# Products of the identity with itself in TensorE's waits, in a two-layer vision tower

## Chip, cores and metric

The kernel runs on one core of one Trainium2 chip. The metric is the device time of one execution in microseconds (us), as the median of several runs. The kernel is one program that computes the whole tower; all stages share one set of engines: TensorE (PE, with its weight loads as PEld), VectorE (DVE), ScalarE (ACT), GpSimd (POOL) and SyncE (SP).

## The reference

64 images of 64x64x3 are cut into 16 patches each, which makes 1024 tokens of width 192. On them:

```
h = patches @ W + b + pos_emb
h = h + attn0(layernorm(h))       # 12 heads of 16, each image attends to its own 16 tokens, softmax, no output matrix
h = h + soft_moe(layernorm(h))    # 4 experts x 256 slots:
    logits   = x @ phi            #   (tokens, 1024 slots)
    dispatch = softmax over the image's 16 tokens; combine = softmax over the 1024 slots
    out      = combine @ mlp_e(dispatch.T @ x)
h = h + attn1(layernorm(h))       # 6 heads of 32, low-rank projections, rotary, causal
h = h + routed_moe(layernorm(h))  # 32 experts in 4 groups, 4 of them per token
```

All of it is in float32. The change touches only the first attention (attn0) and the computation of the slot weights (logits, dispatch and combine).

## The kernel before

**Stages.** `build` writes the stages one behind the other: `embed`, `attention0` (which begins with the layernorm "ln0"), the layernorm "ln1", `slot_weights`, `hidden_pieces`, `slot_experts`, `attention1`, `routed_moe`. Each stage is a block in which every engine has its own written-out list of instructions; the engines meet at the end of a block, so a stage begins when the slowest engine has ended the one before. Within a block the engines wait for each other on counting semaphores. There is no scheduler: the order on an engine is the order in which the code is written. The tokens are handled in 8 tiles of 128 (`TILES`, `P`).

**keep_busy** (line 92) already exists. `keep_busy(pe, g, bank, products)` issues that many float32 products of the 128x128 identity `g.ident` with itself into the first 128 columns of a PSUM bank; nobody reads them (line 95). The kernel before calls it at the start of `embed` (6 products, line 130) and in each layernorm before the transposes (16 products, line 202). In the trace one product is two records, each a weight load and a matmul of 128x128.

**attention0.** TensorE's list is, in order: queries and keys of the first 512 tokens in four parts, each two matmuls of 96x512 (`queries_and_keys(n)`, n = 0 to 3, line 388), with `values(0)` and `values(1)` among them (line 396); `scores(0)`, `scores(1)` (line 408); `values(2)`, `values(3)`; and then a loop over the tiles i = 0 to 7. In the loop stand:

- at i = 0 the parts n = 4 to 7 of the queries and keys of the other 512 tokens;
- `scores(i + 2)`, as long as there is such a tile; at i = 2 `values(4)` to `values(7)` come ahead of it, each of which waits until VectorE has taken the one before out of the only bank for values (`v_done`, line 518);
- `turn(i - 1)` (line 428), three transposes of the outputs of the tile before, after ScalarE has copied them to SBUF (`leave_outputs`, line 474);
- `outputs(i)` (line 419), 12 small products of probabilities and values, which wait for the exponentials of tile i.

After the loop comes `turn(7)`. ScalarE's list is the key copies of a part (`leave(5)`, six activations, line 467) and one query copy (line 464), for each tile four exponentials (line 485), and behind those of tile i the copy of the outputs of tile i-1. VectorE takes the other keys out (`leave(4)`, six operations, line 513), then for each tile the maximum, the subtraction and a transpose (`center`, lines 524 to 531), and at the end of a tile `finish` (lines 536 to 540); GpSimd adds the result to `h` (line 500).

**ln1** is `layernorm(..., wide=True)`: VectorE computes the statistics and `xn`, GpSimd copies 64 columns of each tile once more (line 170), TensorE transposes (line 209), ScalarE copies to `xnT` (line 225).

**slot_weights.** For each tile TensorE computes the logits (`logits`, lines 785 and 789), transposes them into `dl` and, one tile later, the normalised combine weights into `tp` (both line 778). The loop has 9 rounds; `logits(i + 2)` stands at the end of the rounds 0 to 5, and the rounds 6, 7 and 8 have nothing in its place. ScalarE copies `cl` and `tp` out (lines 816 and 835), computes two sets of exponentials (826, 838) and scales one of them (832); GpSimd multiplies the dispatch weights by the inverse sums (877). Then `hidden_pieces` begins, whose first work on TensorE is eight transposes (line 973) and products of 128x384 (lines 979 and 984).

The functions that the change touches:

Of the kernel before, what the change touches and what calls it, by code (L numbers as in the profile page):

```python
# [18 lines left out]
TILES = TOKENS // P  # L19
# [72 lines left out]
def keep_busy(pe, g, bank, products):  # L92

    for _ in range(products):
        pe.matmul(bank[:, 0:P], g.ident[:], g.ident[:], start=True, stop=True)
# [257 lines left out]
def attention0(nc, g, t):  # L353
# [4 lines left out]
    with Scope(nc, "at0") as s:  # L358
# [17 lines left out]
        def _(pe):  # L376
# [15 lines left out]
            def values(i):  # L392
                if i >= 1:
                    pe.wait_ge(v_done, i)
                for k in range(NKD):
                    mm = pe.matmul(vp[:, 0:D], g.xnT[:, k, i * P:(i + 1) * P], t.w[:, k, 2 * D:3 * D],
                                   start=(k == 0), stop=(k == NKD - 1))
                mm.then_inc(v_ready, 1)
# [38 lines left out]
            scores(0)  # L437
            scores(1)
            values(2)
            values(3)  # L440
            for i in range(TILES):
                if i == 0:
                    for n in range(4, 8):
                        queries_and_keys(n)
                if i + 2 < TILES and i != 2:
                    scores(i + 2)
                if i == 2:
                    for j in range(TILES // 2, TILES):
                        values(j)
                    scores(i + 2)  # L450
                if i >= 1:
                    turn(i - 1)
                outputs(i)
            turn(TILES - 1)

        @block.scalar
        def _(act):
# [285 lines left out]
def slot_weights(nc, g, CT, Dn, zn):  # L743


    with Scope(nc, "slw") as s:
# [4 lines left out]
        cl = s.ps("cl", [P, 2, 2, 512])  # L751
# [20 lines left out]
        @block.tensor  # L772
        def _(pe):
            pe.wait_ge(g.phi_in, 16)

            def transposed(bank, src, ready):
                for c in range(SLOT_CHUNKS):
                    tr = pe.transpose(chunks(bank)[:, c, :], src[:, c * P:(c + 1) * P], g.ident[:])
                tr.then_inc(ready, 1)

            def logits(i):
                if i >= 2:
                    pe.wait_ge(lg_ready, i - 1)
                for half in range(2):
                    pe.matmul(cl[:, i % 2, half, :], g.wideT[:, 0, i * P:(i + 1) * P], g.phi[:, half * 512:(half + 1) * 512],
                              start=True, stop=False)
                for half in range(2):
                    rows = slice(half * KQ, (half + 1) * KQ)
                    mm = pe.matmul(cl[:, i % 2, half, :], g.wideT[rows, 1, i * P:(i + 1) * P], g.phi[rows, ALL_SLOTS:],
                                   start=False, stop=True)  # L790
                mm.then_inc(cl_ready, 1)

            logits(0)
            logits(1)
            for i in range(TILES + 1):
                if i < TILES:
                    pe.wait_ge(lg_ready, i + 1)
                    if i >= 1:
                        pe.wait_ge(dsub_ready, i)
                    transposed(dl, lg[:, i % 2], dl_ready)  # L800
                if i >= 1:
                    pe.wait_ge(cw_ready, i)
                    if i >= 2:
                        pe.wait_ge(ct_done, i - 1)
                    transposed(tp, ex[:, (i - 1) % 2], tp_ready)
                if i + 2 < TILES:
                    logits(i + 2)

        @block.scalar
        def _(act):  # L810
# [1098 lines left out]
```

## Time and profile before

| | us |
|---|---|
| median of 3 runs | 1126.56 |
| lowest and highest run | 1112.64, 1131.46 |
| the profiled execution, its device time | 1124.79 |
| its span in the trace | 1123.0 |
| TensorE busy in the span | 996.8 (89%) |
| ScalarE busy | 666.5 (59%) |
| VectorE busy | 390.0 (35%) |
| mean granted clock of TensorE | 0.945 of full speed |

All times inside the program are counted from the start of the span. A row of a timeline gives the start of a group of like instructions, its length, the engine, the source line, the tile that is written and the ones that are read, the number of records, and in brackets how long the engine was idle before and who released it. Stages in this execution, by TensorE's first instruction: the attention's main block 32.3 to 88.9, ln1 to 98.2, slot weights to 155.5, hidden pieces after that.

### The profile page before, as it was taken

The page shows a single profiled execution, that of the slowest core. Times are in us where ns is not written, and L with a number is a line of the kernel's source. Part 1 is how long each engine was busy: PE and PEld are TensorE (multiplying, and loading weights), DVE is VectorE, ACT ScalarE, POOL GpSimd, SP SyncE. Part 2 cuts the span into 40 slices and gives each one's busy share as a digit, 9 for nine tenths or more (in the row PEclk, how much of TensorE's full clock was granted, in tenths as well). Part 3 has the DMA queues.
Part 4 walks back from the last instruction along what each step waited for, and adds up shares of the span by engine and source line. Part 5 has one row for each costly group of instructions (what it writes and reads, how often), then busy time and mean ns, then how long its engine had stood idle before and what let it go on. Part 6 is the DMA issues. An engine that isn't in the chain of part 4 may idle for free. (4 is left out here: it accounts for less than half of the span.)

```text
span 1123.0 us, 21359 instructions
## 1 busy us (share of the span) xinstructions
PE 996.8 (89%) x7464; PEld 653.3 (58%) x7464; DVE 390.0 (35%) x1021; ACT 666.5 (59%) x1226; POOL 257.4 (23%) x256
## 2 busy tenths in 40 slices
PE   8878769779999999999999997875159999999997
PEld 8345445433444445444444445444149999999996
DVE  2555968650011111111111113774832222222233
ACT  0474968679888888788888881262013443334332
POOL 0111233230000000000000000100455555655531
PEclk9888969889999999999999999997569999999999
DMA  9000008979545555445544511004369999999994
GB/s 356 7 1 1 1 30 318 315 315 187 118 114 127 123 118 119 109 121 125 124 112 116 113 29 47 0 1 136 140 224 286 323 328 328 325 320 334 321 267 127
DMA packets 76137, 185.52 MB, mean 165 GB/s; under 512 B 15888, under 2 KB 34544, under 8 KB 75768
## 3 DMA queue, kind: packets, MB, share of 16 engines
q1 hardware_dynamic: 63788, 169.45, 49.5%
q0 software_dynamic: 11808, 14.39, 6.2%
q8 instruction: 64, 1.05, 0.4%
q14 instruction: 45, 0.37, 0.1%
q10 hardware_dynamic: 432, 0.26, 0.1%
HBM read 148.37 MB, written 35.69 MB: 164 GB/s over the span
## 5 line engine op out<-in xcount | busy, mean ns | idle before, releaser
L1182 ACT ACTIVATE sle_H<-sle_hp 128x1024 f32<-128x1024 f32 x384 | 367.5, 1024 | 57.7 <-PE sle_hp L1119 57.6
L1631 ACT ACTIVATE ext_H<-ext_hp,ext_bias 128x128 f32<-128x128 f32 x378 | 103.9, 397 | 162.9 <-issue 159.2
L1136 PE MATMUL sle_up<-sle_H,sle_cw 128*32 128x512 f32 (+1 forms) x2048 | 191.4, 492 | 0.0
L1197 DVE STREAM_TRANSPOSE sle_UT<-sle_up 128x256 f32<-128x256 f32 x64 | 37.3, 583 | 291.7 <-PE sle_up L1136 291.7
L1576 PE MATMUL ext_yp<-rmoe_w,ext_H 128*128 128x192 f32 x756 | 133.5, 326 | 1.1 <-issue 0.6
L1576 PEld LDWEIGHTS ext_yp<-rmoe_w,ext_H 128*128 128x128 f32 x756 | 121.6, 191 | 1.6 <-issue 1.6
L1119 PE MATMUL sle_hp<-keep_G,keep_dT 99*128 99x512 bf16 (+1 forms) x512 | 101.8, 332 | 12.3 <-PEq L897 6.8
L1104 POOL COPY sle_cw<-keep_CT 128x128 f32 (+1 forms) x64 | 18.7, 293 | 393.0 <-PE sle_up L1136 392.9
L1136 PEld LDWEIGHTS sle_up<-sle_H,sle_cw 128*32 128x32 f32 x2048 | 53.5, 109 | 87.0 <-issue 73.4
L1119 PE MATMUL sle_hp<-sle_G,sle_dT 99*128 99x512 bf16 (+1 forms) x512 | 100.0, 327 | 1.1 <-ACT sle_H L1182 1.1
L1558 PE MATMUL ext_hp<-ext_xT,rmoe_w 128*128 128x128 f32 x756 | 97.2, 280 | 0.0
L1119 PEld LDWEIGHTS sle_hp<-keep_G,keep_dT 99*128 99x128 bf16 x512 | 44.8, 99 | 81.7 <-ACT sle_H L1182 31.3
L1558 PEld LDWEIGHTS ext_hp<-ext_xT,rmoe_w 128*128 128x128 f32 x756 | 91.9, 196 | 0.0
L1119 PEld LDWEIGHTS sle_hp<-sle_G,sle_dT 99*128 99x128 bf16 x512 | 44.5, 98 | 69.4 <-ACT sle_H L1182 30.3
L1735 POOL DMA_INDIRECT sum<-ext_y,ext_yi x40 | 63.6, 1589 | 61.7 <-DVE ext_gate L1653 33.5
L1724 POOL DMA_INDIRECT ext_x<-xn,ext_xi x63 | 61.9, 983 | 34.9 <-issue 26.6
L1145 PE MATMUL sle_up<-keep_w,sle_UT 128*128 128x192 f32 x384 | 67.3, 326 | 0.8 <-DVE sle_UT L1197 0.8
L1663 DVE COPY ext_yi<-rmoe_slot 128x1 uint32<-128x1 uint32 x63 | 9.7, 154 | 154.6 <-PE ext_yp L1576 152.2
L1145 PEld LDWEIGHTS sle_up<-keep_w,sle_UT 128*128 128x128 f32 x384 | 61.7, 190 | 2.1 <-DVE sle_UT L1197 1.7
L979 PE MATMUL hid_gps<-pre_w,vit_xnT 128*128 128x384 f32 x128 | 47.2, 512 | 5.7 <-DVE hid_rest L1022 5.7
L1564 PE MATMUL ext_hp<-ext_xT,rmoe_w 64*128 64x128 f32 x756 | 51.4, 283 | 0.0
L999 ACT ACTIVATE hid_gp<-hid_gps 128x768 bf16<-128x768 f32 (+1 forms) x40 | 34.0, 850 | 27.1 <-PE hid_gps L984 14.6
(271 smaller groups left out, 1213.6 us busy)
## 6 DMA issues: line engine op xcount, KB each, us to landing
rmoe_w<-W SPq DMA_DIRECT2D x126, 576.0 KB
pieces<-hid_gp SPq DMA_DIRECT2D x16, 1152.0 KB, 4.8
keep_G<-pieces SPq DMA_DIRECT2D x32, 288.0 KB, 3.9
sle_G<-pieces SPq DMA_DIRECT2D x32, 288.0 KB, 3.8
pieces<-hid_gp SPq DMA_DIRECT2D x8, 768.0 KB, 5.5
keep_G<-pieces SPq DMA_DIRECT2D x32, 192.0 KB, 3.8
sle_G<-pieces SPq DMA_DIRECT2D x32, 192.0 KB, 3.7
keep_CT<-xT SPq DMA_DIRECT2D x6, 512.0 KB, 6.5
```

Of the source, the lines that this page charges most:

```text
L979: pe.matmul(gps[(STEPS * i + e) % 4][:, half, 0:HALF], g.wideT[:, 0, tokens], g.w1[:, e - 1, half * HALF:(half + 1) * HALF], start=True, s ...
L1119: mm = pe.matmul(hp[k % DEEP][:, j, off:off + width], dT[b][:, c * P:(c + 1) * P], G[b][:, (c // 2) * HID + at:(c // 2) * HID + at + width ...
L1136: mm = pe.matmul(to[32 * e:32 * e + 32], cw[:, p, 2 * e + grp, :], H[:, p, h:h + width], start=(p == 0 and grp == 0), stop=(p == 1 and grp ...
L1145: mm = pe.matmul(yps, UT[:, par, b, :], g.w2[:, b, :], start=(b == blocks[0]), stop=(b == blocks[-1]))
L1182: act.activation(H[:, p, WIDTH * k:WIDTH * (k + 1)], hp[k % DEEP][:].rearrange("p a c -> p (a c)"), ACT.Gelu_apprx_tanh).then_inc(gelu_don ...
L1197: dve.transpose(UT[:, par, at // 32:(at + width) // 32, 32 * j:32 * j + 32], src.rearrange("p (b c) -> p b c", c=32)).then_inc(ut_done[ban ...
L1558: pe.matmul(hp[q][:, c % 2, (c // 2) * P:(c // 2 + 1) * P], rt.w1[:, w, c, :], xT[:, q, 0, :], start=(c < 2), stop=False)
L1564: mm = pe.matmul(hp[q][:, c % 2, (c // 2) * P:(c // 2 + 1) * P], rt.w1[rows, w, HC + c // 2, :], xT[rows, q, 1, :], start=False, stop=(c > ...
L1576: mm = pe.matmul(yp[:, 0:D], H[:, q, c, :], rt.w2[:, w, c, :], start=(c == 0), stop=(c == HC - 1))
L1631: act.activation(H[:, q, c, :], hp[q][:, c % 2, (c // 2) * P:(c // 2 + 1) * P], ACT.Gelu, bias=bias[:, q, c:c + 1]).then_inc(gelu_done, 1)
L1724: pool.indirect_dma_start(out=x[:, p, :], out_offset=None, in_=xn_dram, in_offset=bass.IndirectOffsetOnAxis(ap=xi[p][:], axis=0)).then_inc ...
L1735: pool.indirect_dma_start(out=sums[q], out_offset=bass.IndirectOffsetOnAxis(ap=yi[q][:], axis=0), in_=y[:, q, :], in_offset=None, compute_ ...
```

## The change

`keep_busy` is called at further places of two of TensorE's lists. In `attention0`: 9 products between `values(2)` and `values(3)`; 2 behind each of the parts 4, 5 and 6 of the queries and keys; 2 behind each of `values(4)` to `values(7)`; for the tiles 3, 4 and 5 two ahead of `outputs(i)` and two behind it, for the tiles 6 and 7 four and four; 12 behind `turn(7)`. In `slot_weights`: 8 at the end of each of the rounds 6, 7 and 8. The banks written are `oT` before any outputs exist, `qk[0]` once its last content has left, and halves of `cl` that have been read. No wait is added, and the other engines' lists stay as they are. All products are counted here as matmuls; the trace shows two records for each.

```
--- before.py
+++ after.py
@@ -437,21 +437,30 @@
             scores(0)
             scores(1)
             values(2)
+            keep_busy(pe, g, oT, 9)
             values(3)
             for i in range(TILES):
                 if i == 0:
                     for n in range(4, 8):
                         queries_and_keys(n)
+                        if n < 7:
+                            keep_busy(pe, g, oT, 2)
                 if i + 2 < TILES and i != 2:
                     scores(i + 2)
                 if i == 2:
                     for j in range(TILES // 2, TILES):
                         values(j)
+                        keep_busy(pe, g, qk[0], 2)
                     scores(i + 2)
                 if i >= 1:
                     turn(i - 1)
+                if i >= 3:
+                    keep_busy(pe, g, qk[0], 2 if i + 2 < TILES else 4)
                 outputs(i)
+                if i >= 3:
+                    keep_busy(pe, g, qk[0], 2 if i + 2 < TILES else 4)
             turn(TILES - 1)
+            keep_busy(pe, g, qk[0], 12)
 
         @block.scalar
         def _(act):
@@ -805,6 +814,8 @@
                     transposed(tp, ex[:, (i - 1) % 2], tp_ready)
                 if i + 2 < TILES:
                     logits(i + 2)
+                else:
+                    keep_busy(pe, g, cl[:, i % 2, 0], 8)
 
         @block.scalar
         def _(act):
```

On TensorE, in the first attention, from the values of the tiles 2 and 3 to the last part of the queries and keys (`at_w,vit_xnT` are values, `vit_xnT,at_w` queries and keys, `vit_ident` alone the added products):

```order
-L396 MATMUL at_b<-at_w,vit_xnT 128x192 x4
-L388 MATMUL at_b<-vit_xnT,at_w 96x512 x8
+L396 MATMUL at_b<-at_w,vit_xnT 128x192 x2
+L95 MATMUL at_b<-vit_ident 128x128 x9
+L396 MATMUL at_b<-at_w,vit_xnT 128x192 x2
+L388 MATMUL at_b<-vit_xnT,at_w 96x512 x2
+L95 MATMUL at_b<-vit_ident 128x128 x2
+L388 MATMUL at_b<-vit_xnT,at_w 96x512 x2
+L95 MATMUL at_b<-vit_ident 128x128 x2
+L388 MATMUL at_b<-vit_xnT,at_w 96x512 x2
+L95 MATMUL at_b<-vit_ident 128x128 x2
+L388 MATMUL at_b<-vit_xnT,at_w 96x512 x2
```

What stood in one piece is now cut by 9, 2, 2 and 2 products.

On TensorE, the end of the first attention, tiles 6 and 7 (`at_oT` are the transposes of outputs, `at_probT,at_v` the outputs):

```order
 L428 MATMUL at_b<-vit_ident,at_oT 128x128 x3
+L95 MATMUL at_b<-vit_ident 128x128 x4
 L419 MATMUL at_b<-at_probT,at_v 32x128 x12
+L95 MATMUL at_b<-vit_ident 128x128 x4
 L428 MATMUL at_b<-vit_ident,at_oT 128x128 x3
+L95 MATMUL at_b<-vit_ident 128x128 x4
 L419 MATMUL at_b<-at_probT,at_v 32x128 x12
+L95 MATMUL at_b<-vit_ident 128x128 x4
 L428 MATMUL at_b<-vit_ident,at_oT 128x128 x3
+L95 MATMUL at_b<-vit_ident 128x128 x12
```

Every step of the two tiles now has products behind it, and 12 stand at the end of the block.

On TensorE, the last rounds of the slot weights in the changed kernel (the transposes of line 778 before are line 787 here):

```order
L787 MATMUL slw_dl<-vit_ident,slw_lg 128x128 x8
L787 MATMUL slw_tp<-vit_ident,slw_ex 128x128 x8
L95 MATMUL slw_cl<-vit_ident 128x128 x8
L787 MATMUL slw_dl<-vit_ident,slw_lg 128x128 x8
L787 MATMUL slw_tp<-vit_ident,slw_ex 128x128 x8
L95 MATMUL slw_cl<-vit_ident 128x128 x8
L787 MATMUL slw_tp<-vit_ident,slw_ex 128x128 x8
L95 MATMUL slw_cl<-vit_ident 128x128 x8
```

Before, only the five groups of transposes stood there; three groups of 8 products have come in.

## Rows read from the trace of the kernel before

**Rows 1.** The granted clock in 40 slices of the span, tenths of full speed

```profile
PEclk9888969889999999999999999997569999999999
```

**Rows 2.** By stretch: length, busy PE, PEld, DVE, ACT, POOL, then granted clock

```profile
46.20:53.00 6.80, 6.65 (x11) 3.19 (x12) 2.00 (x5) 1.66 (x4) 0.00 (x0) 0.50 0.00 0
...
66.80:73.20 6.40, 6.40 (x63) 3.89 (x63) 2.53 (x6) 1.07 (x3) 0.59 (x1) 0.50 0.01 3
73.50:83.60 10.10, 6.62 (x142) 4.59 (x142) 6.80 (x17) 9.42 (x19) 2.36 (x4) 1.00 0.01 2
83.90:93.90 10.00, 7.48 (x51) 6.50 (x51) 5.63 (x29) 1.98 (x3) 1.25 (x3) 0.50 0.00 0
94.10:141.70 47.60, 39.04 (x194) 21.34 (x192) 37.23 (x55) 41.06 (x90) 11.60 (x13) 1.00 0.00 1
142.00:158.70 16.70, 9.04 (x35) 7.32 (x36) 10.78 (x21) 10.31 (x17) 7.69 (x5) 0.50 0.01 1
```

**Rows 3.** Timeline, TensorE: identity products at the start and in ln0

```profile
3.33 2.93 PE L95 MATMUL emb_acc<-vit_ident 128*128 128x128 f32 x12 [3.33 <-DMA vit_ident<-ident]
...
24.01 3.81 PE L95 MATMUL at_b<-vit_ident 128*128 128x128 f32 x32 [0.93 <-PEq L100]
```

**Rows 4.** Timeline, all engines: second half of queries and keys, first attention

```profile
46.35 1.65 PE L396 MATMUL at_b<-at_w,vit_xnT 96*128 96x192 f32 x4 [2.27 <-DVE at_v L518]
...
51.45 4.40 DVE L513 TENSOR_SCALAR pre_Dn<-at_b,at_bias,at_hm 96x512 f32<-96x512 f32 x6 [3.06 <-PE at_b L388]
...
54.02 4.10 ACT L467 ACTIVATE keep_CT<-at_b,at_kbias,at_hm 96x512 f32<-96x512 f32 x6 [6.09 <-PE at_b L388]
...
55.91 1.96 PE L388 MATMUL at_b<-vit_xnT,at_w 96*96 96x512 f32 x4 [0.21 <-DVE pre_Dn L513]
...
58.57 2.14 ACT L485 ACTIVATE at_probT<-at_turned 32x384 f32<-32x384 f32 x4
```

**Rows 5.** Timeline, all engines: values 4 to 7 of the first attention

```profile
63.92 0.92 PE L396 MATMUL at_b<-at_w,vit_xnT 96*128 96x192 f32 x4 [0.45 <-DVE at_v L518]
...
66.66 1.65 PE L396 MATMUL at_b<-at_w,vit_xnT 96*128 96x192 f32 x4 [0.45 <-DVE at_v L518]
```

**Rows 6.** Timeline, the output of tile 2 leaving, tile 4's outputs

```profile
72.09 0.49 ACT L474 ACTIVATE at_oT<-at_b 128x384 f32<-128x384 f32 x1 [5.99 <-PE at_b L419]
...
76.30 0.86 PE L419 MATMUL at_b<-at_probT,at_v 128*32 128x128 f32 x24
```

**Rows 7.** Timeline, all engines: end of the attention, ln1

```profile
84.00 1.51 PE L419 MATMUL at_b<-at_probT,at_v 128*32 128x128 f32 x24
...
86.12 0.90 PE L428 MATMUL at_b<-vit_ident,at_oT 128*128 128x128 f32 x3 [0.61 <-ACT at_oT L474]
...
87.83 0.59 POOL L500 TENSOR_TENSOR vit_h<-vit_h,at_o 128x192 f32<-128x192 f32 x1 [2.37 <-DVE at_o L540]
...
88.93 6.20 PE L95 MATMUL ln_psT<-vit_ident 128*128 128x128 f32 x32 [1.91 <-PEq L358]
...
93.83 2.27 POOL L170 COPY vit_xn<-vit_xn 128x64 f32<-128x64 f32 x8 [5.41 <-DVE vit_xn L196]
...
94.97 1.91 PE L209 MATMUL ln_psT<-vit_ident,vit_xn 128*128 128x128 f32 x16
```

**Rows 8.** Timeline, all engines: last slot weight tiles, next stage

```profile
142.34 1.97 PE L778 MATMUL slw_dl<-vit_ident,slw_lg 128*128 128x128 f32 x8 [2.66 <-ACT slw_lg L816]
...
150.35 1.94 PE L778 MATMUL slw_tp<-vit_ident,slw_ex 128*128 128x128 f32 x8 [3.82 <-ACT keep_CT L835]
...
153.07 1.93 POOL L877 TENSOR_TENSOR pre_Dn<-pre_Dn,slw_dsum 128x1024 f32<-128x1024 f32 x1 [0.84 <-DVE slw_dsum L849]
...
155.51 1.94 PE L973 MATMUL hid_gps<-vit_ident,pre_Dn 128*128 128x128 f32 x8 [3.22 <-PEq L746]
...
157.24 3.52 PE L979 MATMUL hid_gps<-pre_w,vit_xnT 128*128 128x384 f32 x8
...
167.39 2.75 PE L979 MATMUL hid_gps<-pre_w,vit_xnT 128*128 128x384 f32 x8
```

More of the change, by code:

```diff
@@ L439, in _ @@
             values(2)
+            keep_busy(pe, g, oT, 9)
             values(3)
@@ L444, in _ @@
                         queries_and_keys(n)
+                        if n < 7:
+                            keep_busy(pe, g, oT, 2)
                 if i + 2 < TILES and i != 2:
@@ L449, in _ @@
                         values(j)
+                        keep_busy(pe, g, qk[0], 2)
                     scores(i + 2)
@@ L452, in _ @@
                     turn(i - 1)
+                if i >= 3:
+                    keep_busy(pe, g, qk[0], 2 if i + 2 < TILES else 4)
                 outputs(i)
+                if i >= 3:
+                    keep_busy(pe, g, qk[0], 2 if i + 2 < TILES else 4)
             turn(TILES - 1)
+            keep_busy(pe, g, qk[0], 12)
         @block.scalar
@@ L807, in _ @@
                     logits(i + 2)
+                else:
+                    keep_busy(pe, g, cl[:, i % 2, 0], 8)
         @block.scalar
```

## Prediction

> **What bounds the kernel now.** I read the granted clock first. The slices of the page [rows 1] (28 us each) show it lowest in the sixth, somewhat low in the second to the fourth, eighth and ninth, and low again in the 28th to the 30th, far behind the change. The busy time by stretch [rows 2] then shows the places. The clock has two levels here, 2.4 GHz (1.00) and 1.2 GHz (0.50), and it is at the lower one in 46.2 to 53.0, 66.8 to 73.2, 83.9 to 93.9 and 142.0 to 158.7 us. These are the two stages that the change touches, plus the layernorm and the stage that follow them. In 6.65 of 6.80 us and in 6.40 of 6.40 us of the first two TensorE is busy: there it is the bound and works at half speed. Between them, 73.5 to 83.6, ScalarE is busy in 9.42 of 10.10 us and TensorE in 6.62, so ScalarE is the bound and TensorE's speed costs nothing. I then took the timeline of all engines at each fall and asked what TensorE had done ahead of it, and who waited for it afterwards.
>
> Ahead of the first fall TensorE had been idle 2.27 us [rows 4]; ahead of the second it ran values of 0.92 us with 0.45 us of waiting between them [rows 5]; ahead of the fourth it was idle 2.66 us [rows 8]. In 94.1 to 141.7 the clock held with 39.04 of 47.60 us busy [rows 2]. So the falls follow thinly used stretches, and products in the gaps should prevent some of them.
>
> **Price of a product.** One product is two records. At full clock 16 take 3.81 us, 0.11 us of which are the last one's tail: 0.23 us each. At half clock 6 take 2.93 us: 0.46 us each [rows 3]. The change adds 63 products in the attention and 24 in the slot weights, 87 x 0.23 = 20 us of TensorE. What counts is how many of them stand where nobody waits for TensorE.
>
> **Step 1, queries and keys.** The nine products take 9 x 0.23 = 2.05 us of the 2.27 us gap [rows 4]: hidden. If the clock holds, the work from 46.35 until ScalarE starts on part 5 at 54.02 (7.67 us, 6.65 of it at half clock [rows 2]) shrinks by 3.3 us, and the pair of products behind part 4 gives 0.46 back: -2.9. ScalarE has 4.10 us of key copies there and goes on straight to the exponentials at 58.57 [rows 4], on which the tiles 0 and 1 hang, so all of it arrives at tile 2. VectorE's six operations (4.40 us from 51.45) begin some 2.5 us earlier, half of the 5.1 us behind 46.35, and part 7 on TensorE, which waits for them (55.91), with them; its result is not the last that tile 1 waits for. The other end: if the clock falls nonetheless, nine products cost 4.1 us in a gap of 2.27 and the pair 0.9, so +2.7.
>
> **Step 2, values 4 to 7.** The pair behind each of the first three values (0.46) fills the gap of 0.45 [rows 5]: nothing. From values(7) at 66.66 to ScalarE's copy of the outputs of tile 2 at 72.09 [rows 5, 6] there are 5.43 us in which TensorE has no wait (values, scores, turn, outputs) and ScalarE is idle 5.99 us. At full clock they are half, 2.7, and the last pair adds 0.5: -2.2. At half clock all pairs would cost 0.46 more each: +2.
>
> **Step 3, tiles 3 to 5.** TensorE is busy 6.62 of 10.10 us while ScalarE's list is nearly full [rows 2]. ScalarE needs 2.14 + 0.49 = 2.63 us a tile [rows 4, 6], and with handing over 2.7; TensorE 6.62 / 10.10 x 2.7 = 1.8, in a tile with scores up to 2.0. Four products add 0.91: 2.7 to 2.9. The cover is just used up. I take +0.1 a tile, +0.3 (0 to 0.6).
>
> **Step 4, the end of the attention.** Here nothing covers them. For tile 6: +0.15 of its eight products show, since it has no scores. Tile 7: four products ahead of outputs(7) +0.91; outputs(7) at full clock 0.86 in place of 1.51 -0.65 [rows 6, 7]; the four behind it nearly fit in ScalarE's copy, +0.14. Then the block's end: before, from turn(7) at 86.12 to GpSimd's end at 88.42 are 2.30 us [rows 7]; after, TensorE itself ends last, 0.45 of turn plus 12 x 0.23 plus tail 0.1 = 3.3: +1.0. Sum +1.5 (1.3 to 1.7 at full clock).
>
> **Step 5, ln1.** Its 16 products take about 6 us, mostly at half clock, and the first transposes start at 94.97, though GpSimd's first copy was there at about 94.1 [rows 7]. At full clock the 16 take 3.8 us as in ln0 [rows 3] and the transposes go by GpSimd's copies, which end at 96.10: -0.7, of the 0.8 by which they begin earlier (0 if the clock has fallen).
>
> **Step 6, slot weights and the next stage.** In the last tiles nobody waits for TensorE: GpSimd ends the stage at 155.0, out of VectorE's chain, and the next begins at 155.51 [rows 8]. What the low clock costs is in the next stage: eight transposes take 1.94 us and would take half, eight products of 128x384 3.52 against 2.75 later on [rows 8], 1.7 us together. Do the products hold the clock? The first eight fill 1.8 of the 2.66 us. The second eight stand behind tile 6's transposes (issued at about 144.6, 1.0 us at full clock) and end at 147.4; the next transposes start at 150.35 because of ScalarE. A gap of 2.95 us stays, longer than both gaps ahead of which the clock fell, so I expect a fall there. Then the last eight run at half clock, 152.3 to 155.9, and hold up the end of the stage by 0.9; but TensorE is then busy without a pause from 150.35, 5.6 us, and in 88.93 to 93.9 five such us brought the clock back [rows 2, 7]. So -1.7 + 0.9, about -0.7 with a little off for a late rise. Ends: -1.7 (no fall) and +0.9 (it does not come back in time). I take -0.7, nearest to the row of ln1.
>
> On that gap the Trainium skill speaks, in "TensorE: Matmul & The Clock Gate", section "Why this matters for your kernels": throughput drops mid-kernel are put down to single long idle gaps between bursts. The trace does not bear this out alone, since the gaps right ahead of the second fall were 0.45 us each [rows 5]. By the page the 2.95 us are just within what is allowed, the clock would hold, step 6 would be -1.7 and the time 1 us less.
>
> **Sum.** -2.9 -2.2 +0.3 +1.5 -0.7 -0.7 = -4.7 us. The profiled execution took 1124.79, so 1120.1; that execution is 1.8 below the median of the three runs, 1126.56, whose runs lie between 1112.64 and 1131.46. I let the gain carry through: the stages behind work on what this program has computed, so they move forward with it. A measurement of this kernel can tell about 2% (22 us) from no change, so this is far inside.
>
> **Rivals.**
> - *The falls only move.* The products stand in some gaps and not in others: tiles 0 and 1 have none, though TensorE waits for ScalarE there too. If one of the two falls in steps 1 and 2 is put off rather than avoided, its gain (2.2 to 2.9) goes and the rest stays: the time is 1124.79 - 2 to 1124.79, say 1123.5. For it: the second fall came without a long gap. Against: the pairs sit exactly in the stretch ahead of it. 22%.
> - *Slower: the clock falls in the last tiles of the attention, as it did at 83.9, and the products stand on the path at double price.* There TensorE ends the block. From outputs(7) at 84.00 on [rows 7], against before, which had the low clock too: the four products ahead +1.8; the four behind 1.8 less the 0.61 us of waiting there, +1.2; twelve 5.5 in place of the 1.4 us from the end of turn(7) at 87.02 to GpSimd's end at 88.42, +4.1. That is +7.1 in place of the +1.5 of step 4, so 1125.7; a fall in tiles 3 to 5 adds 2.7 us for each tile that it covers (TensorE's 1.8 doubled, plus 1.8 for four products, against 2.7), one or two of them: 1130. It decides as soon as the clock is low for one of these tiles. Against: at full clock TensorE is then busy nearly all of the time, more than in 94.1 to 141.7, where the clock held. 13%.
> - *Products do not count for the clock at all*, so all falls stay and steps 1, 2 and 4 take their upper ends: above 1135. The clock came back during ln1's products, at about 94, which speaks against it. 2%.
> - *More than forecast:* a low stretch in a later stage (the slices 28 to 30 [rows 1]) or part of it falls away because everything is shifted in time, 1110 to 1115. 3%.
>
> **How the numbers follow.** Forecast 60%: 1120.1. Its own bounds with all unknown terms at their good end are -0.3 -1.0 -0.2 = 1118.6. Below that I leave the scatter of the runs of before, half of 1131.46 - 1112.64, 9.4: 1109. Above, the range takes in the slower rival at 1130 and the highest run: 1131.5.  Faster by over 2% (under 1104) 2%, slower by over 2% (over 1149) 1%, within 97%.
>
> **What would show it.** In the changed profile: the granted clock at 1.00 from 24 to about 143 us. Nine products end before values(3); ScalarE's key copies of part 5 begin 2.9 us earlier; outputs of tile 2 leave 5 us earlier, near 67. Exponentials of tiles 4 to 7 come every 2.7 to 2.8 us. ln1's first instruction comes at about 85.6, released by TensorE's list and not by GpSimd's; the slot weights begin near 94.3. The clock falls between 143 and 147, and the last eight products at 0.46 each. It is wrong if the clock is at 0.50 anywhere in 46 to 86, or if tiles 3 to 5 take more than 2.9 us each.

## Result and profile after the change

The changed kernel takes 1133.83 us (median of 4 runs, 1133.06 to 1138.17); on the same chip the kernel before took 1126.99 (4 runs, 1112.64 to 1131.46). The ratio is 1.0104 with a 95% interval of 1.0057 to 1.0151: slower by 1.0%, inside the 2% that I called no change, but on the other side of the forecast of 1120.1 and above its range, which ended at 1131.5. The profiled execution took 1134.2 us (span 1132.4), that of before 1124.79 (span 1123.0).

First, where are the 9.4 us of span? I cut both traces at the first TensorE instruction of each stage. The first attention is counted from the products of its own layernorm, at 24 us, and the slot experts up to their last multiplication:

| stage | before, us | after, us | difference |
|---|---|---|---|
| first attention | 64.9 | 63.0 | -1.9 |
| ln1 | 9.3 | 8.8 | -0.5 |
| slot weights | 57.3 | 57.3 | 0 |
| hidden pieces | 91.2 | 90.0 | -1.2 |
| slot experts | 436.4 | 447.0 | **+10.6** |
| second attention | 89.8 | 91.7 | +1.9 |
| routing | 48.4 | 47.3 | -1.1 |
| routed experts | 296.1 | 297.2 | +1.1 |
| end | 5.5 | 6.1 | +0.6 |

The part that the prediction worked out (the first four rows) gained 3.6 us. Then the slot experts, in which no line has been changed, took 10.6 us more. The busy times by stretch say of what kind. The columns are start:end and length, then busy time (and instructions) of PE, PEld, DVE, ACT and POOL, the granted clock, the share of the DMA engines and GB/s. The changed kernel, from the first attention to the slot experts:

```profile
24.00:87.00 63.00, 57.95 (x583) 41.49 (x583) 36.53 (x94) 34.92 (x66) 8.80 (x11) 1.00 0.07 28
87.00:95.70 8.70, 6.17 (x48) 5.23 (x48) 6.32 (x31) 3.82 (x10) 2.27 (x8) 1.00 0.01 2
95.70:153.00 57.30, 46.48 (x240) 28.50 (x240) 45.57 (x64) 48.32 (x97) 15.47 (x9) 0.97 0.00 1
153.00:243.00 90.00, 77.21 (x321) 41.45 (x322) 63.62 (x69) 63.09 (x81) 28.18 (x18) 0.95 0.79 290
243.00:690.00 447.00, 434.71 (x3455) 204.78 (x3456) 59.44 (x121) 368.53 (x385) 20.61 (x66) 0.98 0.49 113
```

The same stretches of the kernel before:

```profile
24.00:88.90 64.90, 50.93 (x456) 30.02 (x457) 36.49 (x93) 34.94 (x66) 8.76 (x11) 0.85 0.07 29
...
246.70:683.20 436.50, 428.99 (x3456) 203.78 (x3456) 59.47 (x121) 368.54 (x385) 20.60 (x66) 1.00 0.51 116
```

In the attention the clock is now at 1.00 throughout (before, 0.85). In the slot experts TensorE does the same 3456 multiplications but is busy 5.7 us longer (434.71 against 428.99) and idle 4.8 us longer. Both numbers have a place. This is TensorE's timeline at the first of two such places in the changed kernel:

```profile
450.27 0.61 PE L1130 MATMUL sle_hp<-sle_G,sle_dT 99*128 99x256 bf16 x3
452.99 0.61 PE L1130 MATMUL sle_hp<-keep_G,keep_dT 99*128 99x512 bf16 x3 [2.11 <-issue]
453.53 1.05 PE L1147 MATMUL sle_up<-sle_H,sle_cw 128*32 128x256 f32 x9
457.51 1.93 PE L1147 MATMUL sle_up<-sle_H,sle_cw 128*32 128x512 f32 x7 [2.93 <-issue]
459.37 1.89 PE L1130 MATMUL sle_hp<-keep_G,keep_dT 99*128 99x512 bf16 x5
```

And the same instructions in the kernel before:

```profile
454.02 0.61 PE L1119 MATMUL sle_hp<-sle_G,sle_dT 99*128 99x256 bf16 x3
457.02 0.61 PE L1119 MATMUL sle_hp<-keep_G,keep_dT 99*128 99x512 bf16 x3 [2.38 <-issue]
457.55 1.50 PE L1136 MATMUL sle_up<-sle_H,sle_cw 128*32 128x256 f32 x16
458.98 1.47 PE L1119 MATMUL sle_hp<-keep_G,keep_dT 99*128 99x512 bf16 x8
```

Both show one pause of 2.1 to 2.4 us here, "issue", with nothing in the profile to wait for. It stands where the loop of this stage jumps back: `slot_experts` writes 16 images out and runs the other 48 in three laps of 16, so two jumps. The branch at the end of a lap has records of its own on TensorE's sequencer. In the kernel before (shortest, median and longest in ns, first and last start in us):

```profile
L1070 PEldq COMPARE_BRANCH  x3: 83/3402/3913, 452.8 to 670.1; - x3
```

At the two jumps it takes 3.9 and 3.4 us, at the end of the loop, where nothing jumps, 0.08. The branches of the other engines on the same line take 0.04 to 0.07 us each.

Only the changed kernel has a second pause, 2.93 us, twelve multiplications later, in the middle of a group of 16. It comes at both jumps:

```profile
567.40 0.60 PE L1130 MATMUL sle_hp<-keep_G,keep_dT 99*128 99x512 bf16 x3 [2.13 <-issue]
...
571.64 1.93 PE L1147 MATMUL sle_up<-sle_H,sle_cw 128*32 128x512 f32 x7 [1.95 <-issue]
```

2.93 + 1.95 = 4.88 us are the idle time. The rest is the clock: it is at 1.2 GHz for 6.8 us each from 455.5 and from 568.1 (seven of the group take 1.93 us there, where all sixteen took 1.50), and those are the 5.7 us of longer busy time. Together 10.6.

What could stop an engine in the middle of a group that waits for nothing? The page of the profile has a queue named "instruction". Its rows (packets, MB, share) of the changed kernel and of the kernel before:

```profile
q8 instruction: 68, 1.11, 0.4%
```

```profile
q8 instruction: 64, 1.05, 0.4%
```

1.11 MB in 68 packets and 1.05 in 64 are 16.4 KB a packet (each is 16,384 bytes in the trace): the program comes in blocks. In the 16 us around the first jump (446 to 462) the changed kernel's queue has 4 packets; in the 13 us around it (449 to 462) that of before has 2. Measured from the start of the branch, the changed kernel's packets begin at +1.1 us and at +5.3; TensorE goes on at +3.9, begins the last multiplication that it has at +4.9 and goes on again at +8.4, 3.5 us later.

**Theory P (place):** after a jump back the block behind the one that was jumped to is requested only when the engine runs again, and takes some 3 us. If the place to which the loop jumps lies shortly ahead of a block's end, TensorE eats the rest of that block before the next is there, and waits a second time. The 87 products are 348 instructions (two weight loads and two multiplications each; the page counts 21707 against 21359) and have moved the loop's start by as much. Blocks begin at fixed places, so the shift counts by what is left over whole blocks. By 64 bytes an instruction, which the Trainium skill states in "Perfetto Trace Analysis", section "The 4-stage abstract model", a block of 16,384 bytes holds 256, and 348 leave 92; the runs below test that number.

**Rivals:** the products, in the attention or in the slot weights, cost the time themselves, through the clock or some other state that they leave; and the second pause has nothing to do with place but with when this stage starts.

### The profile page after: what moved, and what is told of

It reads as the page before. It is cut to its first block and busy times, and to the rows that moved or that the text cites. A ratio compares the mean times of both kernels' runs of the same rounds, so it can differ in the third digit from the quotient of the medians.

```text
span 1132.4 us, 21707 instructions
## 1 busy us (share of the span) xinstructions
PE 1011.6 (89%) x7638; PEld 666.9 (59%) x7638; DVE 389.8 (34%) x1021; ACT 666.6 (59%) x1226; POOL 257.5 (23%) x256
## 3 DMA queue, kind: packets, MB, share of 16 engines
q8 instruction: 68, 1.11, 0.4%
## 5 line engine op out<-in xcount | busy, mean ns | idle before, releaser
L1147 PE MATMUL sle_up<-sle_H,sle_cw 128*32 128x512 f32 (+1 forms) x2048 | 195.2, 496 | 4.9 <-issue 4.9
```

The source lines that it names most:

```text
L1147: mm = pe.matmul(to[32 * e:32 * e + 32], cw[:, p, 2 * e + grp, :], H[:, p, h:h + width], start=(p == 0 and grp == 0), stop=(p == 1 and grp ...
```

## Experiments

The kernels with waits only repeat a wait that has long been met. Times are medians with the lowest and highest and the number of runs, and are compared only with the kernel before on the same chip, since chips differ (the routed experts alone took 296 to 298 us in the runs 1 to 8, on two chips, and 288 to 290 in the runs 9 to 14, on a third). Two tables at the end of this section put the profiles side by side.

**Only the attention's products** (252 instructions, 4 short of a block of 256). The change without:

```
-                else:
-                    keep_busy(pe, g, cl[:, i % 2, 0], 8)
```

> The 63 products of the first attention alone, the 24 of the slot weights left out. Theory P (place of the code): the changed kernel lost 10.5 us in the slot experts, which the change does not touch, because 348 more TensorE records (87 products x 4) stand ahead of the loop of that stage and move its first instruction close to the end of one of the 16384-byte blocks in which TensorE's instructions are fetched; after each of the two jumps back TensorE then runs dry a second time. 63 products are 252 records, nearly a whole block of 256, so the loop start lies as in the kernel before: no second stall, slot experts 436.5 us from first to last product as before, attention and ln1 3.0 us shorter, total about 1124. Rival T (time of the start, or a transfer that collides): the slot experts suffer whenever they begin some us earlier; then this kernel also loses about 10 us there, total near 1133.

1126.73 us (1124.51 to 1130.51, 10 runs), before 1123.26 (1114.86 to 1128.39, 25): 1.0032 [1.0002, 1.0061]. Slot experts 437.7 us, one pause a jump. The attention's products do not cause the 10.6 us.

**Only the slot weights' products** (96 instructions). The kernel before with only those two lines.

> The 24 products of the slot weights alone. Theory P: 96 records shift the loop start by nearly the same rest as the whole change (348 - 256 = 92), so the second stall after each jump back is there, 10 us in the slot experts, total about 1136. Rival T: the slot experts begin less than 1 us earlier than before, so nothing is lost there, total about 1126. Rival C (the products' own clock effect in the attention is what costs later): no loss either.

1138.36 (1137.48 to 1140.85, 4 runs): 1.0126 [1.0055, 1.0197]. Slot experts 449.0 us, second pause ten multiplications behind the first:

```profile
457.61 0.61 PE L1121 MATMUL sle_hp<-keep_G,keep_dT 99*128 99x512 bf16 x3 [2.57 <-issue]
458.15 0.80 PE L1138 MATMUL sle_up<-sle_H,sle_cw 128*32 128x256 f32 x7
461.86 2.29 PE L1138 MATMUL sle_up<-sle_H,sle_cw 128*32 128x256 f32 x9 [2.91 <-issue]
```

Taken alone this fits both P (96 left over, near 92) and a rival by which the slot weights' products are to blame. The next run parts them.

**No product at all, only the shift.** The kernel before, with this at the end of TensorE's list in `hidden_pieces`; an instruction holds two waits, so 184 waits are 92 instructions. The page counts 21452 against 21359, 93 more: the last one is a branch at the end of that block, of which the kernels with waits show a record and the kernel before does not. Whether it is one instruction more was not settled; it would move the place by half a multiplication.

```
+            for _ in range(184):
+                pe.wait_ge(g.w1_in, 16)
```

> The kernel before with 184 waits on a count that was reached long ago (92 instructions, two waits each) at the end of TensorE's list in the hidden pieces, where TensorE is idle for 6.8 us; no product is added and nothing computed changes. Theory P: a shift of 92 instructions as in the whole change, so two stalls more in the slot experts, 5 us each, total about 1137, with no change in any other stage. Rival T and rival C: no difference from the kernel before, 1127.

1136.19 (1130.24 to 1142.11, 10 runs): 1.0090 [1.0055, 1.0125]. This is the decisive one: not one product, 92 instructions that do nothing, and the loss of the whole change is there. The second pause stands behind the same twelfth multiplication, at both jumps:

```profile
451.23 1.92 PE L1138 MATMUL sle_up<-sle_H,sle_cw 128*32 128x256 f32 x9
454.51 1.93 PE L1138 MATMUL sle_up<-sle_H,sle_cw 128*32 128x512 f32 x7 [1.36 <-issue]
...
568.85 1.93 PE L1138 MATMUL sle_up<-sle_H,sle_cw 128*32 128x512 f32 x7 [2.12 <-issue]
```

and the stage is as long as in the changed kernel:

```profile
240.00:687.50 447.50, 436.49 (x3456) 204.95 (x3456) 59.47 (x121) 368.56 (x385) 20.61 (x66) 0.98 0.49 113
```

It also shows a period: 92 instructions do what 348 do, 256 more.

**The whole change, shifted on.** The changed kernel with `range(96)` of the same waits, 48 instructions more: 396, which leave 140.

> The changed kernel with 96 waits on a count that was reached long ago (48 instructions) at the same place. Theory P: the loop start, about 40 instructions ahead of the end of its fetch block in the changed kernel, moves into the next block and has nearly a whole block ahead of it; the second stall goes, the slot experts take 436 us and the gain of 3.7 us in the stages ahead is seen: total about 1122. Rival T or C: still 1133.

1125.74 (1122.85 to 1132.55, 10 runs): 1.0029 [0.9998, 1.0061]. The second pause is gone and so are the 10 us, with all 87 products in place:

```profile
452.32 0.60 PE L1132 MATMUL sle_hp<-keep_G,keep_dT 99*128 99x512 bf16 x3 [2.32 <-issue]
...
561.19 0.60 PE L1132 MATMUL sle_hp<-keep_G,keep_dT 99*128 99x512 bf16 x3 [2.38 <-issue]
```

```profile
242.10:679.00 436.90, 428.86 (x3456) 203.74 (x3456) 59.50 (x121) 368.50 (x385) 20.80 (x66) 1.00 0.50 116
```

**No jump.** If jumps back cost the pauses, the stage without a loop has neither. The kernel before, and then the changed one, with:

```
-    BODY = 2 * TILE_IMAGES
+    BODY = IMAGES
...
-            with eng.Fori(1, IMAGES // BODY) as r:
-                for m in range(BODY):
-                    image(BODY * r + m, m, r, False)
```

> The kernel before with the loop of the slot experts written out for all 64 images, so that no engine jumps back. Theory P: in the kernel before each of the two jumps back costs one stall of TensorE of 1.9 to 2.4 us plus some ramp, so the stage takes 431 to 432 us in place of 436.4 and the total is about 1119 on the scale of the kernel before's 1123 to 1127. Rival: longer code costs more elsewhere (more fetches in a straight line), and nothing is gained.

> The same for the changed kernel. Theory P: both stalls at each jump go, so the slot experts take as long as in e5_before_no_loop (431 to 432 us, against 447.0) and the kernel is 13 to 15 us faster than the change. What is left between this kernel and e5 is what the products are worth by themselves: by the stages' times of one profile each -3.7 us; but a look at e3 showed an attention of the kernel before without a single fall of the clock, 58.2 us from its first product to ln1 where 64.9 was my base and 63.0 is the changed kernel's, so averaged over executions I expect the products to be worth between -2 and +3 us. Rival T (an earlier start costs the slot experts 10 us): this kernel stays 10 us above e5.

Before without the loop 1119.73 (1115.70 to 1122.23, 8 runs), the change without it 1118.73 (1117.96 to 1121.49, 6 runs), before 1126.66 (1118.64 to 1129.68, 19): 0.9947 [0.9919, 0.9975] and 0.9940 [0.9913, 0.9967]. The slot experts take 431.8 us in both, so the two ordinary pauses with what follows them cost some 5 us of 436.4, and the change has no cost there once there is no jump. The rows are those of before, then those of the change:

```profile
240.50:672.30 431.80, 428.89 (x3455) 204.05 (x3456) 59.43 (x121) 368.26 (x385) 20.70 (x66) 0.99 0.52 117
```

```profile
243.70:675.50 431.80, 428.66 (x3455) 203.99 (x3456) 59.42 (x121) 368.28 (x385) 20.59 (x66) 0.99 0.53 117
```

**The front products only, in a good place.** Of the change the first 23 products (nine, three pairs in the queries and keys, four pairs at the values; those of tiles 3 to 7, of the block's end and of the slot weights are left away), and the 96 waits: 92 + 48 = 140 instructions.

> The first 23 of the 87 products alone (nine ahead of values(3), the pairs in queries and keys and in the values), with 48 instructions of waits that put the loop start well into a fetch block (92 + 48 = 140). If the products of tiles 3 to 7 and the twelve at the end are what the change pays for the clock, the attention takes 59 to 61 us from its first product to ln1 in place of 63.0, the slot experts 436.5, the total 1119 to 1123. If the clock falls in the attention without the later products, it takes 62 and nothing is won over e1 (1126.7).

1126.73 (1121.51 to 1130.36, 10 runs): 1.0005 [0.998, 1.003]. The attention takes 60.4 us, less than the 63.0 with all products. There is no second pause, as P says for 140, and yet the slot experts took 440.8 us and not 436.9: the clock fell for 3.4 us at the end of each jump's only pause (454.5 and 563.8). The first run and the eighth have one such fall at one of their two jumps, which accounts for the 1.3 and 1.5 us that they are above 436.4. Why here at both and not in the fourth run, with the loop at the same place, is open.

**The kernel before once more**, for its spread in the trace.

> One look at the kernel before once more. If the place of the falls of the clock differs from execution to execution, its attention takes 58 to 65 us from its first product to ln1 and the falls stand elsewhere than at 46, 67 and 84 us; if the falls belong to the program, it repeats 64.9 with falls within a microsecond of the same places.

One run: 1128.12 us, slot experts 437.9, attention 63.9, with a fall of 3.4 us at 87.8 where the first profile has one of 10.2 at 83.7 [rows 2].

**Two other shifts.** The kernel before with 120 and with 224 waits, 60 and 112 instructions. By P the pause moves by one multiplication for two instructions: 16 later for 60, 10 earlier for 112.

> The kernel before with 60 instructions of waits in the idle end of the hidden pieces, 32 fewer than in e3. Theory P in numbers: after a jump back the first block is asked for at +1.0 us, TensorE goes on at +4.2, the next block is asked for at +5.2 and serves from about +8.4. With 92 instructions TensorE ran dry after 12 more matmul records; with 60 it should get some 26 to 28 records further, dry at about +7, and wait 1 to 1.5 us in place of 2.4 to 3.5. If the stall does not depend on the distance but comes or goes as a whole, it is 2.4 to 3.5 us again or nothing.

> The same with 112 instructions, 20 more than in e3. Theory P: only 2 to 6 matmul records are left behind the jump, so TensorE runs dry at about +4.5 and waits 3.5 to 4 us until the next block at about +8.4; slot experts 448 to 452 us. If the stall comes or goes as a whole: as in e3, 447.5.

One run each: 1118.76 and 1132.76 us, with before at 1118.62 on this chip. For 60 the pause stands 27 multiplications behind the restart and is short, 1.03 us at both jumps, because it begins later and ends as long after the jump as the others; the clock there holds, and the stage takes 438.6:

```profile
457.43 1.50 PE L1138 MATMUL sle_up<-sle_H,sle_cw 128*32 128x256 f32 x16
458.86 1.47 PE L1121 MATMUL sle_hp<-keep_G,keep_dT 99*128 99x512 bf16 x8
461.36 1.50 PE L1138 MATMUL sle_up<-sle_H,sle_cw 128*32 128x256 f32 x16 [1.03 <-ACT sle_H L1184]
```

For 112 it stands 3 behind the restart and is long, 3.72 and 3.32 us, and the stage takes 448.7. (This kernel's total also holds 2.1 us of the waits themselves: its 112 wait instructions run from 235.3 to 247.3 us, 0.107 us each, longer than TensorE's idle time there, and the slot experts begin that much later.)

```profile
458.18 0.84 PE L1121 MATMUL sle_hp<-keep_G,keep_dT 99*128 99x512 bf16 x3 [2.12 <-issue]
462.74 2.79 PE L1138 MATMUL sle_up<-sle_H,sle_cw 128*32 128x256 f32 x16 [3.72 <-issue]
```

12, 27 and 3 against 12, 28 and 2: the place of the pause is what P makes of the shift. (The trace names ScalarE as the releaser of the 1.03 us. The length of a pause behind an "issue" or a named engine says little here; its place says more.)

**What the products are worth with no jump behind them.** Without the loop the change can be judged by itself. Twice on one chip: the front 23 products without the loop, and then, in one go, before, all products, and the front 23, each without the loop.

> The first 23 products of the attention with the slot experts' loop written out. The attention takes 60 to 61 us (60.4 in e7, 63.0 with all products, 58.2 to 58.5 in undisturbed executions without any, 64 to 65 in disturbed ones), the slot experts 431.8 us. If the products up to the values pay, the total is 1117 to 1119, up to 2 us under e5 (1119.7) and e6 (1118.7); if their price and the clock they save cancel, it is 1119 to 1120. Either way below both the kernel before and the change.

> The kernel before without the loop, on one chip with the next two, so that nothing differs between the three but the products. Its attention should take 58 to 59 us in some executions and 64 to 65 in others, by where the clock falls. If executions of the two kinds are about equally frequent, its median is within 1.5 us of e13 and its spread is wider. If disturbed ones are the rule, it is 2 us slower than e13.

> The change without the loop. Attention 63.0 us in every execution; spread smaller than that of e12. If my first sum had been right but for the loop, it would be 4.7 us under e12; from the stages' times I expect -2 to +1.

> The first 23 products alone, without the loop. Attention 59.3 to 60.4 us, so 2.6 to 3.7 under e13; ln1 and the stage behind the slot weights up to 1.5 us longer than with all products where the clock is low there. So 1 to 3 us under e13, and 1 to 3 under e12. If the products of the last tiles pay after all, it is level with e13.

| without the loop | median (range, runs) | to before with its loop |
|---|---|---|
| front 23, first call | 1109.88 (1107.03 to 1112.80, 12) | 0.9933 [0.9911, 0.9955] |
| no products | 1112.71 (1107.49 to 1120.62, 12) | 0.9962 [0.9933, 0.9992] |
| all 87 | 1110.23 (1107.46 to 1112.44, 12) | 0.9939 [0.9913, 0.9965] |
| front 23 again | 1110.58 (1105.55 to 1112.93, 12) | 0.9931 [0.9905, 0.9956] |

Before took 1118.62 (17 runs) and 1118.37 (28). All four are below the kernel before on the same chip. The products' own worth is 1112.71 - 1110.23 = 2.5 us by the medians, but the intervals overlap, and on the chip of the runs 5 to 8 it was 1.0 us, so it is not shown. The spread is narrower: 13.1 us without products, 5.0 with all, 5.8 and 7.4 with the front 23; 6.5 and 3.5 in the fifth and the sixth run.

All kernels by what the shift leaves over 256, with the slot experts' time in their profiled execution:

| left over 256 | kernel | slot experts, us | second pause |
|---|---|---|---|
| 0 | before; again | 436.4; 437.9 | none |
| 60 | 120 waits | 438.6 | 27 behind the restart, 1.03 us |
| 92 | **the change**; 184 waits | 447.0; 447.5 | 12 behind |
| 96 | slot weights only | 449.0 | 10 behind |
| 112 | 224 waits | 448.7 | 3 behind, 3.72 us |
| 140 | change + 96 waits; front + 96 waits | 436.9; 440.8 | none |
| 252 | attention only | 437.7 | none |
| no jump | five of the six kernels; all products again | 431.8; 432.4 | no pause at all |

Whether a kernel has products or not does not show in this column; its place does. Nor does the start of the stage, the other rival: it begins at 243.0 us in the change and at 242.1 in the fourth run, at 246.1 with the slot weights' products only and at 246.7 before.

**The same order of events at every jump.** The ten profiles with a loop have 20 jumps. Counted from the branch, the first packet begins at +0.9 to +1.6 us, TensorE goes on at +3.7 to +4.5, and the next packet begins at +4.9 to +6.1, in good places as in bad ones. The ten second pauses all end at +7.9 to +8.6, wherever they began. A good place is one in which TensorE has enough instructions left until then.

**The clock at the jumps.** At the eight jumps with a second pause of 1.36 us or more it was at 1.2 GHz for 6.8 or 10.2 us every time; at the two with one of 1.03 us it held; at the ten without a second pause it fell four times, for 3.4 us each. In the run with 184 waits the first of these falls began at 449.8, ahead of the second pause, so the second pause alone does not bring them all.

And the first attention, in every profiled execution:

| products in the attention | its length, us |
|---|---|
| none (8 profiles) | 64.9, 63.9, 64.9, 64.9, 64.9, 58.2, 58.5, 61.1: mean 62.7 |
| front 23 (3) | 60.4, 59.3, 59.1: mean 59.6 |
| all 63 (5) | 63.0, 63.1, 63.0, 63.0, 63.0 |

## Why the prediction was wrong

**The step that failed** is the sentence under the sum: "I let the gain carry through: the stages behind work on what this program has computed, so they move forward with it." They moved forward by 3.7 us (3.6 from the stages of the table), and there the loss began. The step put the effect of 348 inserted instructions on the stages behind at nothing. 10.6 us arose at two jumps of a loop that the change does not touch, because inserted instructions push all later code on; about 4.8 us of it was waiting and 5.7 a lower clock. With its 92 left over it was just ahead of a block's end; 44 to 48 instructions more and it is not (the fourth run). None of the rivals was this one; three were about the clock in the stages with products, and the fourth looked behind them, but for a gain. That the slower rival named 1130 and carried the range to 1131.5 is no merit of it: its fall in the tiles did not happen, the attention ran at 1.00. One row of before held the hint and I did not read it: the two pauses of 2.38 and 1.87 us at the jumps, "issue", and the queue named instruction. Of 348 inserted instructions one should have asked what else they move than the clock.

**The step that was right in kind and wrong in reference:** the 4.7 us were taken against one execution of before, with three falls in the attention and ln1 [rows 2]. The same attention code took 58.2 us in another profile, that of the 184 waits, with no fall in it at all:

```profile
22.60:80.70 58.10, 43.47 (x456) 26.27 (x456) 36.39 (x93) 34.91 (x65) 8.76 (x11) 1.00 0.10 41
```

So with all products the attention saves 1.9 us against a profile with the falls, and loses 4.8 against this one; against the mean of eight, 62.7, it is 0.3 longer. The sum should have weighed both.

The steps one by one, cut at ScalarE's copies of the outputs (tile 2 and tile 5) in the two profiles. In the changed kernel and, below, in the kernel before, where that of tile 2 is at 72.09 [rows 6]:

```profile
67.24 0.49 ACT L483 ACTIVATE at_oT<-at_b 128x384 f32<-128x384 f32 x1 [4.05 <-PE at_b L419]
...
76.51 0.49 ACT L483 ACTIVATE at_oT<-at_b 128x384 f32<-128x384 f32 x1 [0.47 <-PE at_b L419]
```

```profile
80.17 0.49 ACT L474 ACTIVATE at_oT<-at_b 128x384 f32<-128x384 f32 x1
```

- *Steps 1 and 2, queries, keys and values:* right. No fall in 24 to 143. ScalarE's key copies of part 5 began at 51.12, 2.9 us earlier, as forecast. The outputs of tile 2 began on TensorE at 66.31, ScalarE took them at 67.24 (forecast near 67), 4.9 us earlier than before [rows 6]; forecast 5.1.
- *Step 3, tiles 3 to 5:* mis-sized. Forecast 2.7 to 2.9 us a tile, +0.3 in all. From the copy of tile 2 to that of tile 5 it took 9.27 us in place of 8.08, +1.2; a tile settles at 3.15 us for 2.70. That is over the 2.9 us that the prediction itself named as a sign of being wrong. TensorE's list in the changed kernel:

```profile
69.29 0.86 PE L419 MATMUL at_b<-at_probT,at_v 128*32 128x128 f32 x24
70.08 0.71 PE L95 MATMUL at_b<-vit_ident 128*128 128x128 f32 x4
70.72 0.53 PE L408 MATMUL at_b<-pre_Dn,at_qT 98*32 98x192 f32 x8
71.07 0.51 PE L408 MATMUL at_b<-keep_CT,at_qT 98*32 98x192 f32 x8
71.51 0.55 PE L428 MATMUL at_b<-vit_ident,at_oT 128*128 128x128 f32 x3
71.90 0.61 PE L95 MATMUL at_b<-vit_ident 128*128 128x128 f32 x4
...
73.87 0.53 PE L408 MATMUL at_b<-pre_Dn,at_qT 98*32 98x192 f32 x8
```

  None of these rows has a wait, and ScalarE now waits for TensorE (0.47 us at 76.51): TensorE bounds these tiles. A pair takes 0.54 (71.90 to 72.44, where the outputs begin) or 0.64 us (70.08 to 70.72), not twice 0.23 [rows 3]: beside multiplications of 32 columns it does not run at the pace of a long row of its own kind. And TensorE's own work is 3.15 - 0.54 - 0.64 = 1.97 us, the upper of my two figures.
- *Step 4, the end of the attention:* about right. From the copy of tile 5 to ln1 it took 10.47 us (76.51 to 86.98) in place of 8.76 (80.17 to 88.93), +1.7 for +1.5. Against the front 23 products alone, the 40 products of steps 3 and 4 cost 63.0 - 59.6 = 3.4 us by the mean, and 4.0 against the one of the three profiles with no fall in the attention (59.1). At the end, as forecast, TensorE itself finishes last: the twelve products end at 86.68.

```profile
83.52 0.49 PE L428 MATMUL at_b<-vit_ident,at_oT 128*128 128x128 f32 x3
83.84 2.84 PE L95 MATMUL at_b<-vit_ident 128*128 128x128 f32 x24
86.98 3.81 PE L95 MATMUL ln_psT<-vit_ident 128*128 128x128 f32 x32 [0.30 <-PEq L358]
```

  These answer to [rows 7]. ln1 begins at 86.98; forecast 85.6.
- *Step 5, ln1:* -0.5 for -0.7. Its 16 products take 3.81 us in place of 6.20.
- *Step 6, slot weights:* right about the gap, the fall and the gain behind; 0.9 us too dear for the last eight products. These rows answer to [rows 8]:

```profile
147.88 1.56 PE L787 MATMUL slw_tp<-vit_ident,slw_ex 128*128 128x128 f32 x8 [2.92 <-ACT keep_CT L846]
149.23 3.14 PE L95 MATMUL slw_cl<-vit_ident 128*128 128x128 f32 x16
153.04 1.07 PE L984 MATMUL hid_gps<-vit_ident,pre_Dn 128*128 128x128 f32 x8 [0.67 <-PEq L755]
153.94 2.75 PE L990 MATMUL hid_gps<-pre_w,vit_xnT 128*128 128x384 f32 x8
```

  The gap that I put at 2.95 us is 2.92, and the clock fell behind it, at 148.3 (forecast 143 to 147), but for 3.4 us only. The last eight products took 3.14 us and still ended ahead of GpSimd (152.4 and 152.5), so the stage kept its 57.3 us where the forecast had +0.9. The next one began at full clock, 1.07 for 1.94 and 2.75 for 3.52, 1.6 us together for the forecast 1.7, and was 1.2 shorter as a whole; step 6 in all -1.2 for -0.7. The Trainium skill ("TensorE: Matmul & The Clock Gate", section "Why this matters for your kernels") puts such drops down to long idle gaps; by it the clock would have held over 2.92 us, as the prediction said. It did not here. In the changed kernel without the loop (sixth run) the fall came at 142.3, ahead of this gap, so the gap alone does not explain it either.
- *A reading:* the lowest slice of [rows 1] is the 29th, 0.5, not the sixth, 0.6. Nothing in the sum rests on it.

From 24 to the start of the slot experts that makes -4.8 + 1.2 + 1.7 - 0.5 - 1.2 = -3.6 us for -4.7. The second attention's +1.9 and the routed experts' +1.1 have not been looked into; over all profiles the second attention takes between 89.7 and 97.7 us, so 1.9 is within what the code does by itself. Over the executions the loss is smaller than in the one profile: 1133.83 - 1126.99 = 6.8 us.

**What stays open.** That the block is requested late is read from the times of the packets and from how the pause moves with the shift; the mechanism inside the chip was not seen. Why the clock fell at the only pause of a jump in four cases and not in six, and why the same attention has three falls in one execution and none in another, is not settled. And on one chip the kernels in a good place are 0.3% slower than before (1.0032 and 1.0029, the first just clear of no change), while without the loop the change is ahead of its counterpart by 0.1 to 0.2%: whether the products bring anything to the median was not decided.

## What to carry to other kernels

Ahead of any edit that adds or removes instructions, look for loops behind it. Behind each jump back, look for a pause marked "issue" and, a few multiplications on, for a second one in the middle of a group. If a stage that nobody touched has changed its time, shift it with a few dozen empty waits before blaming the edit; here 48 of them were worth 10 us and writing the loop out gave the best kernels of all (1110.2 with the products, against 1118.4 before on the same chip). And before a sum is built on falls of the clock in one profile, take a second profile of the same kernel: of eight, four had the attention at 64.9 us and two at 58.2 and 58.5. Products that keep TensorE busy belong where it waits, not into tiles in which they use up all the time that it has to spare.

## What the runs showed of the hardware

- TensorE's program comes in packets of 16.4 KB. A jump back costs TensorE a pause of 1.87 to 2.70 us at the 20 jumps of the ten profiles, wherever it stands, about 5 us for two with all that hangs on it (431.8 us against 436.4).
- A loop that starts shortly ahead of a block's end costs a second pause, 1.03 to 3.72 us. With one of 1.36 us or more the clock was down too, at all eight such jumps: then two jumps cost 10.6 to 12.6 us more (447.0 to 449.0 against 436.4). The places repeat after 256 instructions in the two pairs tried (348 and 92, 396 and 140), and only from over 60 to under 140 left over was it dear in the places tried.
- An instruction with two waits that have been met takes TensorE's sequencer 0.107 us (92 from 228.9 to 238.8 us, 112 from 235.3 to 247.3). Where TensorE is idle as long anyway, it costs nothing: 60 and 92 of them ended 4.2 and 1.2 us ahead of the next stage's first multiplication; 112 held it up by 2.1 us.
- An identity product takes 0.23 us in a row of its kind and 0.27 to 0.32 ahead of and behind multiplications of 32 columns (pairs of 0.54 and 0.64 us), all at 2.4 GHz.
